# Output projection as three products of halves instead of one float32 product, in a transformer block on one core

## The chip, the cores and the metric

The kernel runs on one core of a Trainium2 chip. The metric is the device time of one execution in microseconds (us), lower is better. A core has five engines with a queue each: TensorE (PE; its weight loads are listed as PEld), VectorE (DVE), ScalarE (ACT), GpSimd (POOL) and SyncE (SP), which only starts DMAs here. Engines wait for each other by semaphores; every engine runs its own instructions in the order of the program.

## The reference, cut to what matters

Four sequences of 512 tokens with 128 channels pass an attention block and then a mixture of 160 experts. The change touches the last product of the attention, `a @ o_w.T`.

```python
h = _layernorm(x) * (1 + ca) + sa                       # x: 4 x 512 x 128
qkv = (h @ qkv_w.T).reshape(B, S, 3, 16, 64)            # 16 heads of 64
scores = einsum('bhqd,bhkd->bhqk', q, k) * scale + bias # relative-position bias
attn = softmax(scores, axis=-1)
a = einsum('bhqk,bhkd->bhqd', attn, v)
a = a.transpose(0, 2, 1, 3).reshape(B, S, 16 * 64)
x = x + ga * (a @ o_w.T)                                # the output projection
h = _layernorm(x) * (1 + cb) + sb
x = x + gb * experts(h)                                 # router, top 8 of 160, shared expert
```

## The kernel before, in words

The kernel has two stages. The attention takes the first half of the span, the experts the second; the change is in the attention.

The attention works on pairs of heads. For a sequence `b` there are eight pairs `n` (`HPAIRS`), and each pair has eight units `u` (`UNITS`): two heads by four tiles of 128 queries. One unit is a 128x512 tile of scores. Its way is: `scores` on TensorE (L409, L411) into one of two PSUM banks; `add_bias` on VectorE (L975), which takes the bias from `strips`, writes `prob` and the row minimum `nmax`; `exponential` on ScalarE (L706); `invert_sums` on VectorE (L992), for two units at a time; `normalise` on GpSimd (L858); `transpose_probs` on TensorE (L420); and a copy out of PSUM into `PT` (`copy_unit`, L204), by ScalarE for even units and by VectorE for odd ones. When the eight units of a pair are in `PT`, `attend` (L433) multiplies them by `v_sb`: a(n) in four steps `kb`, the result (128 rows of two heads, 512 tokens) standing in the one bank `BANK_O`. VectorE copies it to `oT` (`copy_o`, L998), and `project_out` (L446) adds its product with `woT[:, hp, :]` to `BANK_Y`. After the last pair of a sequence, `gate_y`, `transpose_y`, `update_x` and `new_statistics` bring the sum into `x_all`.

Nothing plans the order: it is written out by hand, one function `pair(b, n)` on each engine, and each engine's list is a program of its own. All lists overlap three pairs. In the list of `pair(b, n)`, by engine (S = scores, A = attend, T = transpose_probs, V = project_v, QK = project_qk, O = project_out; the numbers are units or steps `kb`):

- TensorE: S0 S1 of n | A2 A3 of n-2 | T4 T5 of n-1 | S2 S3 | V | O of n-2 | T6 T7 of n-1 | S4 S5 | A0 A1 of n-1 | T0 T1 of n | S6 S7 | QK of n+2 | T2 T3 of n.
- VectorE: bias 0, 1 | copy_o of n-2 | copy 5 of n-1 | sums 0 | bias 2, 3 | copy 7 of n-1 | sums 2 | bias 4, 5 | copy 1 | sums 4 | bias 6, 7 | copy 3 | sums 6 | qk_low (L958).
- ScalarE: exp 0, 1 | copy 4 of n-1 | exp 2, 3 | copy_v (L719) | copy 6 of n-1 | exp 4, 5 | copy 0 | exp 6, 7 | qk_high (L702) | copy 2.

Waits that touch the change: A0 of a pair waits until its units 6 (ScalarE) and 7 (VectorE) are copied and until `BANK_O` has been read (`s_o`). O waits for `s_o`. In `pair(b, 2)` of the second to fourth sequence, VectorE's `update_x` (L1018) and `new_statistics` (L1010) of the sequence before stand in the list ahead of `copy_o`.

The kernel has a number format that TensorE takes in one instruction per product, `float32r` (in the profile `fp32r`), beside plain float32, for which one product is two instructions in the profile. Where it is used, each operand is split into a rounded half and a rest, HIGH and LOW, and three products of halves are added (`PASSES`); the projections of q, k, v and the experts are done so already, with ScalarE writing HIGH and VectorE writing LOW as source minus HIGH. The output projection and `attend` are in plain float32.

In the notation of the profile, L446 is the output projection's matmul, L383 QK, L394 V, L998 `copy_o`.

Of the kernel before, what the change touches and what calls it, by code (L numbers as in the profile page):

```python
# [19 lines left out]
F32 = mybir.dt.float32  # L20
F32R = mybir.dt.float32r
# [3 lines left out]
P = 128  # L25
B, S, D = 4, 512, 128
# [8 lines left out]
HPAIRS = H // 2  # L35
# [4 lines left out]
HIGH, LOW = 0, 1  # L40
PASSES = ((HIGH, HIGH), (HIGH, LOW), (LOW, HIGH))


BANK_PROJ, BANK_S, BANK_T, BANK_O, BANK_Y = 0, 2, 4, 6, 7
# [11 lines left out]
def adaln_block(nc, x, emb, qkv_t, o_t, router_t, expert_bias, gate_t_in, down_t, gate_shared_t,  # L56
# [12 lines left out]
    with ctx:  # L69
        def sb(name, shape, dt=F32):  # L70
            return ctx.enter_context(nc.sbuf_tensor(name, shape, dt))

        def sem(name):
            return ctx.enter_context(nc.semaphore(name))

        ps = ctx.enter_context(nc.psum_tensor("ps", [P, 8, 512], F32))
# [1 line left out]
        ident = sb("ident", [P, P])  # L78
        x_all = sb("x_all", [P, B, QT * D])
        wT = sb("wT", [P, 2, QKV], F32R)  # L80
        woT = sb("woT", [P, HPAIRS, D])
        hT = sb("hT", [P, B, 2, S], F32R)
        hcur = sb("hcur", [P, 2, S], F32R)
        strips = sb("strips", [P, H * STRIP])
# [10 lines left out]
        v_sb = sb("v_sb", [P, 2, QT, 4 * HD])  # L95

        prob = sb("prob", [P, UNITS, S])
        oT = sb("oT", [P, 2, S])
        yT = sb("yT", [P, S])
        nmax = sb("nmax", [P, UNITS])  # L100
        rsum = sb("rsum", [P, UNITS])
# [50 lines left out]
        ld = {n: sem("ld_" + n) for n in ("ident", "c", "wmod", "emb", "onehot", "x0", "x", "qkv0", "qkv1", "ow",  # L152
                                          "small", "row", "strips0", "strips1", "strips2", "strips3", "strips4", "hcur")}
# [11 lines left out]
        s_s, s_ttr, s_exp, s_t = sem("scores"), sem("biased"), sem("exped"), sem("transposed")  # L165
        s_ca, s_cd = sem("copied_by_act"), sem("copied_by_dve")
        s_v, s_vc, s_pv = sem("v_projected"), sem("v_copied"), sem("pv_done")
        s_rinv, s_prob, s_o = sem("sums_inverted"), sem("normalised"), sem("o_copied")
        s_ymm, s_yg, s_ytr, s_x2 = sem("y_added"), sem("y_gated"), sem("y_transposed"), sem("x_updated")


# [50 lines left out]
        def _(sp):  # L222
# [54 lines left out]

            stack_pair(0, 0)
            load_strips(1)
            sp.dma_start(woT[:, :, :], o_t.rearrange("(n p) d -> p n d", p=P)).then_inc(ld["ow"], 16)  # L280
            stack_pair(0, 1)
            load_strips(2)
            load_strips(3)
# [64 lines left out]
        def _(pe):  # L348
# [3 lines left out]
            for half in range(2):  # L352
                nc.tensor.matmul(ps[0:H, BANK_PROJ + half, :], emb_sb, onehot[:, half * 512:(half + 1) * 512],
                                 start=True, stop=True).then_inc(row_mm, 1)
# [3 lines left out]
            for j in range(6):  # L358
                last = nc.tensor.matmul(ps[:, BANK_O, j * B:(j + 1) * B], wmod_sb[:, j * D:(j + 1) * D], cS[:, :],
                                        start=True, stop=True)  # L360
# [80 lines left out]
            def project_out(b, n):  # L441
                hp = n % HPAIRS
                pe.wait_ge(s_o, b * HPAIRS + (n + 1))
                if hp == 0:
                    pe.wait_ge(s_x2, b + (n // HPAIRS + X2_AHEAD))
                nc.tensor.matmul(ps[:, BANK_Y, :], woT[:, hp, :], oT[:, n % 2, :], start=hp == 0,  # L446
                                 stop=hp == HPAIRS - 1, skip_group_check=True).then_inc(s_ymm, 1)

            def transpose_y(b):

# [54 lines left out]
            pair(0, 0)  # L505
            pair(0, 1)
            pe.wait_ge(w_split, 6)
            pe.wait_ge(ld["ow"], 16)
            for b in range(B - 1):
                for n in range(2, HPAIRS + 2):  # L510
                    pair(b, n)
# [147 lines left out]
            for b in range(B):  # L659
# [3 lines left out]
                for t in range(QT):  # L663
                    last = nc.tensor.transpose(ps[:, BANK_G + b % 2, t * P:(t + 1) * P], hw[:, b, t * P:(t + 1) * P],
                                               ident[:, :])
# [4 lines left out]
        def _(act):  # L670
# [14 lines left out]
            def first_high(n):  # L685

                b = FIRST_ORDER[n]
                act.wait_ge(full_done, n + 1)
                nc.scalar.copy(hcur[:, HIGH, :] if b == 0 else hT[:, b, HIGH, :], h_full[b]).then_inc(grp_high, 1)
# [8 lines left out]
            def qk_high(b, n):  # L698
                act.wait_ge(s_qk, b * HPAIRS + (n + 1))
                if n >= 1:  # L700
                    act.wait_ge(s_stack[(n - 1) % 2], b * STACKED + PAIR_STACKED * ((n - 1) // 2 + 1))
                nc.scalar.copy(qkH[:, :, :], ps[:, BANK_PROJ:BANK_PROJ + 2, :]).then_inc(s_qkh, 1)  # L702
# [6 lines left out]
            def copy_probs(b, n, u):  # L709
                act.wait_ge(s_t, b * G + (UNITS * n + u + 1))  # L710
                if u == 0 and n >= 2:
                    act.wait_ge(s_pv, b * HPAIRS + (n - 1))
                copy_unit(nc.scalar.copy, n, u).then_inc(s_ca, 1)

            def copy_v(b, i):

                act.wait_ge(s_v, b * HPAIRS + (i + 1))
                half = i % 2
                nc.scalar.copy(v_sb[:, (i // 2) % 2, 2 * half:2 * half + 2, :].rearrange("p t n -> p (t n)"),  # L719
                               ps[:, BANK_PROJ + half, :]).then_inc(s_vc, 1)  # L720

            def pair(b, n, final=False):

                exponential(b, n, 0)
                exponential(b, n, 1)
                if n == 0:
                    qk_high(b, 1)
                if n >= 1:
                    copy_probs(b, n - 1, 4)

                exponential(b, n, 2)
                exponential(b, n, 3)
                if n == 0:
                    copy_v(b, 0)
                if not (final and n >= HPAIRS - 1):
                    copy_v(b, n + 1)
                if n >= 1:
                    copy_probs(b, n - 1, 6)

                exponential(b, n, 4)  # L740
                exponential(b, n, 5)
                if n == 0:
                    first_high(2)
                    first_high(3)
                copy_probs(b, n, 0)

                exponential(b, n, 6)
                exponential(b, n, 7)
                if not (final and n >= HPAIRS - 2):
                    qk_high(b, n + 2)  # L750
                copy_probs(b, n, 2)
# [11 lines left out]
                    pair(b, n)  # L763
            for n in range(2, HPAIRS):
                pair(B - 1, n, True)
            copy_probs(B - 1, HPAIRS - 1, 4)
            copy_probs(B - 1, HPAIRS - 1, 6)


            deviation(slice(0, NT), 3)  # L770
# [97 lines left out]
        def _(dve):  # L868
# [51 lines left out]
            def first_low(n):  # L920
                b = FIRST_ORDER[n]
                modulated_low(n, hcur if b == 0 else hT[:, b, :, :], h_full[b])
# [57 lines left out]
            def copy_probs(b, n, u):  # L980
                dve.wait_ge(s_t, b * G + (UNITS * n + u + 1))
                if u == 1 and n >= 2:
                    dve.wait_ge(s_pv, b * HPAIRS + (n - 1))
                copy_unit(nc.vector.tensor_copy, n, u).then_inc(s_cd, 1)
# [6 lines left out]
                    dve.wait_ge(s_prob, b * G + (g - UNITS + 2))  # L991
                nc.vector.reciprocal(rinv[:, u:u + 2], rsum[:, u:u + 2]).then_inc(s_rinv, 1)  # L992

            def copy_o(b, n):
                dve.wait_ge(s_pv, b * HPAIRS + (n + 1))
                if n >= 2:
                    dve.wait_ge(s_ymm, b * HPAIRS + (n - 1))
                nc.vector.tensor_copy(oT[:, n % 2, :], ps[:, BANK_O, :]).then_inc(s_o, 1)  # L998

            def gate_y(b):  # L1000

# [18 lines left out]
            def pair(b, n, final=False):  # L1020

                add_bias(b, n, 0)
                add_bias(b, n, 1)
                if n == 0:
                    first_low(1)
                    qk_low(b, 1)
                if n == 2 and b >= 1:
                    update_x(b - 1)
                    new_statistics(b - 1)
                if n >= 2:  # L1030
                    copy_o(b, n - 2)
                if n >= 1:
                    copy_probs(b, n - 1, 5)
                invert_sums(b, n, 0)

                add_bias(b, n, 2)
                add_bias(b, n, 3)
                if n == 0:
                    modulate(2)
                    modulate(3)  # L1040
                if n >= 1:
                    copy_probs(b, n - 1, 7)
                invert_sums(b, n, 2)

                add_bias(b, n, 4)
                add_bias(b, n, 5)
                if n == HPAIRS + 1:
                    gate_y(b)
                if n == 0:
                    qkv_low(3)  # L1050
                    qkv_low(4)
                    qkv_low(5)
                copy_probs(b, n, 1)
                invert_sums(b, n, 4)

                add_bias(b, n, 6)
                add_bias(b, n, 7)
                if n == 0:
                    first_low(2)
                    first_low(3)  # L1060
                copy_probs(b, n, 3)
                invert_sums(b, n, 6)
                if not (final and n >= HPAIRS - 2):
                    qk_low(b, n + 2)
# [13 lines left out]
                    pair(b, n)  # L1078
            for n in range(2, HPAIRS):
                pair(B - 1, n, True)  # L1080
            copy_o(B - 1, HPAIRS - 2)
            copy_probs(B - 1, HPAIRS - 1, 5)
            copy_probs(B - 1, HPAIRS - 1, 7)
            copy_o(B - 1, HPAIRS - 1)
            gate_y(B - 1)
            update_x(B - 1)
            new_statistics(B - 1)
# [3 lines left out]
            for n in range(NT):  # L1091
                last = nc.vector.bn_aggr(mv[:, n, :], stats[:, n, :])
# [144 lines left out]
```

## Time and profile before

| | us |
|---|---|
| median of 3 runs | 1002.72 (1000.67 to 1008.64) |
| profiled execution, its own time | 999.45 |
| profiled execution, span | 997.2 |
| PE busy in the span | 946.7 (95%) |
| DVE busy | 767.4 (77%) |
| ACT busy | 678.3 (68%) |
| POOL busy | 398.2 (40%) |

The span is the time between the first and the last instruction that the profiler saw, and 2.25 us of the execution lie around it. Busy times are unions of instructions, and matmuls overlap each other, so that a busy PE is not necessarily at its peak. The attention ends at about 505 us, the experts run from about 550 us to the end.

### The profile page before, as it was taken

The numbers are of one execution on the slowest core, as the hardware profiler recorded it, in microseconds if no ns is written. First come the engines' busy times: TensorE is split into PE (matmuls) and PEld (weight loads), VectorE is DVE, ScalarE is ACT, GpSimd is POOL, SyncE is SP. The second block draws the span as 40 slices with busy tenths as digits, with TensorE's granted clock in tenths as the row PEclk, the third lists the DMA queues.
The fourth block names the chain that finished last, engine by engine and source line by source line (L and its number), as shares of the span: only waits on it lengthen the run. The fifth ranks groups of instructions, "written<-read, shape, count | busy, mean of one in ns | idle before, by whom it ended". The sixth has DMA issues, their size and how long they took to land.

```text
span 997.2 us, 15699 instructions
## 1 busy us (share of the span) xinstructions
PE 946.7 (95%) x4592; PEld 685.8 (69%) x4592; DVE 767.4 (77%) x1452; ACT 678.3 (68%) x1168; POOL 398.2 (40%) x260
## 2 busy tenths in 40 slices
PE   4889999999999999999979699999999999999997
PEld 2546666666666666666524578888888888888886
DVE  5757667766676666767546689999999999999997
ACT  4656666666666666666536577777777777777775
POOL 0668888888888888888800000000000000000000
PEclk9999999999999999999979899999999999999999
DMA  7985445445553564355002999999999999999991
GB/s 210 274 224 125 97 118 127 117 95 128 128 120 81 117 149 110 82 128 127 22 0 75 213 218 221 220 220 223 222 221 225 221 222 223 222 222 222 222 208 43
DMA packets 71105, 160.57 MB, mean 161 GB/s; under 512 B 10272, under 2 KB 36192, under 8 KB 60944
## 3 DMA queue, kind: packets, MB, share of 16 engines
q1 hardware_dynamic: 71056, 159.97, 71.2%
q8 instruction: 24, 0.39, 0.2%
q14 instruction: 25, 0.20, 0.1%
HBM read 105.60 MB, written 2.42 MB: 108 GB/s over the span
## 4 chain that ended last, share of the span: by engine, by line
PE 84%; DMA 5%; DVE 4%; ACT 2%; POOL 2%; SPq 1%; issue 1%; POOLq 0%; ACTq 0%; DVEq 0%
PE ps L620 40%; PE ps L433 11%; PE ps L420 10%; PE ps L409 5%; PE ps L411 5%; PE ps L383 4%; PE ps L446 2%; PE ps L394 2%; POOL prob L858 2%; DMA strips<-in_L_ffn_w_down 2%; DMA k_low<-qk 2%; DVE prob L975 1%; DMA strips<-comb_rows 1%; DMA comb_rows<-strips 1%; PE ps L538 1%
## 5 line engine op out<-in xcount | busy, mean ns | idle before, releaser
L858 POOL TENSOR_SCALAR prob<-prob,rinv 128x512 f32<-128x512 f32 x256 | 398.1, 1568 | 96.4 <-DVE rinv L992 94.3
L706 ACT ACTIVATE prob<-prob,nmax 128x512 f32<-128x512 f32 x256 | 182.9, 715 | 139.5 <-DVE nmax L975 139.5
L620 PE MATMUL ps<-hT,wT 128*128 128x512 f32 x960 | 243.9, 390 | 0.3 <-DVE wT L1144 0.3
L1163 DVE TENSOR_TENSOR PT<-v_sb,strips 128x1024 f32<-128x1024 f32 x160 | 195.9, 1224 | 43.1 <-ACT v_sb L830 29.3
L830 ACT ACTIVATE v_sb<-ps 128x1024 f32<-128x1024 f32 x160 | 164.4, 1028 | 65.2 <-PE ps L620 65.1
L620 PE MATMUL ps<-stack,wT 128*128 128x512 f32 x640 | 198.4, 392 | 9.5 <-DVE wT L1150 9.5
L620 PEld LDWEIGHTS ps<-hT,wT 128*128 128x128 f32 x960 | 180.5, 188 | 38.9 <-ACT strips L805 1.1
L1150 DVE TENSOR_TENSOR wT<-PT,stack 128x1024 fp32r<-128x1024 f32 x160 | 195.0, 1219 | 0.0
L204 DVE COPY PT<-ps 128x512 f32<-128x512 f32 x128 | 88.5, 691 | 137.9 <-PE ps L420 135.2
L822 ACT CAST stack<-PT 128x1024 fp32r<-128x1024 f32 x160 | 166.6, 1041 | 9.5 <-DVE PT L1163 9.5
L420 PEld LDWEIGHTS ps<-ident,prob 128*128 128x128 f32 x1024 | 114.4, 140 | 75.9 <-POOL prob L858 50.9
L975 DVE CUSTOM_DVE_ANT_0 prob<-ps,strips 128x512 f32<-128x512 f32 x256 | 164.5, 680 | 2.7 <-PE ps L411 2.1
L620 PEld LDWEIGHTS ps<-stack,wT 128*128 128x128 f32 x640 | 120.1, 189 | 36.7 <-DVE wT L1150 12.1
L420 PE MATMUL ps<-ident,prob 128*128 128x128 f32 x1024 | 137.2, 276 | 2.8 <-ACT PT L204 1.6
L433 PE MATMUL ps<-PT,v_sb 128*64 128x512 f32 x512 | 124.4, 607 | 4.3 <-ACT PT L204 3.4
L409 PE MATMUL ps<-stack 128*128 128x512 f32 x256 | 112.7, 440 | 6.0 <-DMA k_low<-qk 5.8
L620 PE MATMUL ps<-wT 128*128 128x512 f32 x320 | 98.9, 391 | 0.0
L204 ACT COPY PT<-ps 128x512 f32<-128x512 f32 x128 | 74.0, 578 | 19.1 <-PE ps L420 19.0
L433 PEld LDWEIGHTS ps<-PT,v_sb 128*64 128x64 f32 x512 | 31.5, 137 | 64.7 <-issue 49.7
L620 PEld LDWEIGHTS ps<-wT 128*128 128x128 f32 x320 | 60.3, 189 | 12.6
L409 PEld LDWEIGHTS ps<-stack 128*128 128x128 f32 x256 | 48.8, 191 | 13.0 <-issue 4.0
L817 ACT CAST wT<-strips 128x256 fp32r<-128x256 f32 x80 | 32.3, 405 | 34.1 <-DMA strips<-in_L_ffn_w_down 33.9
(105 smaller groups left out, 742.8 us busy)
## 6 DMA issues: line engine op xcount, KB each, us to landing
strips<-comb_rows SPq DMA_DIRECT2D x158, 512.0 KB, 12.3
stack<-qk SPq DMA_DIRECT2D x128, 256.0 KB, 3.9
k_low<-qk SPq DMA_DIRECT2D x64, 128.0 KB, 3.9
hT<-qk SPq DMA_DIRECT2D x64, 128.0 KB, 3.8
strips<-bias_rows SPq DMA_DIRECT2D x3, 1792.0 KB, 14.7
strips<-in_L_ffn_w_gate SPq DMA_DIRECT2D x80, 64.0 KB, 10.4
strips<-in_L_ffn_w_down SPq DMA_DIRECT2D x80, 64.0 KB, 12.3
strips<-bias_rows SPq DMA_DIRECT2D x2, 896.0 KB, 5.3
```

The source lines that it names most:

```text
L204: return copy(dst[:, :, qt * P:(qt + 1) * P], ps[:, BANK_T + u % 2, :].rearrange("p (k s) -> p k s", s=P))
L409: nc.tensor.matmul(ps[:, BANK_S + g % 2, :], stack[:, par, head, 0, qt * P:(qt + 1) * P], stack[:, par, head, 1, :], start=True, stop=False)
L420: last = nc.tensor.transpose(ps[:, BANK_T + u % 2, kb * P:(kb + 1) * P], prob[:, u, kb * P:(kb + 1) * P], ident[:, :])
L433: last = nc.tensor.matmul(ps[head * HD:(head + 1) * HD, BANK_O, :], v_sb[:, (n // 2) % 2, kb, (n % 2) * P + head * HD:(n % 2) * P + (head ...
L620: last = nc.tensor.matmul(ps[:, bank + c, :], weights(a), rows(m, c), start=start and k == 0, stop=stop and k == 2, skip_group_check=True)
L706: nc.scalar.activation(prob[:, u, :], prob[:, u, :], ACT.Exp, bias=nmax[:, u:u + 1], scale=-1.0, accum_out=rsum[:, u:u + 1]).then_inc(s_ex ...
L822: nc.scalar.copy(h_high[:, k % 4, :], weighted[:, k % 4, :]).then_inc(s_hh, 1)
L830: nc.scalar.activation(silu[:, k % 2, :], ps[:, BANK_G + 2 * half:BANK_G + 2 * half + 2, :].rearrange("p c s -> p (c s)"), ACT.Silu).then_ ...
L858: nc.gpsimd.tensor_scalar(prob[:, u, :], prob[:, u, :], rinv[:, u:u + 1], None, ALU.mult).then_inc(s_prob, 1)
L975: nc.vector.tensor_tensor_reduce(out=prob[:, u, :], in0=ps[:, BANK_S + u % 2, :], in1=backwards, scale=-1.0, scalar=3.0e38, op0=ALU.add, o ...
L1150: nc.vector.tensor_tensor(h_low[:, k % 4, :], weighted[:, k % 4, :], h_high[:, k % 4, :].bitcast(F32), ALU.subtract).then_inc(s_hl, 1)
L1163: nc.vector.tensor_tensor(weighted[:, k % 4, :], silu[:, k % 2, :], cb[:, r, half * HALF:(half + 1) * HALF], ALU.mult).then_inc(s_mul, 1)
```

## The change

The attention's output is no longer copied out of `BANK_O` by VectorE alone. ScalarE writes the rounded half, `oT[.., HIGH, ..]` (`o_high`), and VectorE, when that is there, writes `BANK_O` minus that half (`o_low`). The weights of the projection are split in the same way, once, in `pair(0, 1)`, from the staging tile `o_in`. `project_out` becomes three matmuls in the rounded format. `o_high` stands in ScalarE's list of a pair after exp 1 and ahead of copy 4; `o_low` takes the place of `copy_o`. TensorE no longer waits for the load of the weights but, once, for their split. The size given for the DMAs' scratch memory in the constructor is 4096.

```diff
-        woT = sb("woT", [P, HPAIRS, D])
+        o_in = sb("o_in", [P, HPAIRS * D])
+        wo_parts = sb("wo_parts", [P, 2, HPAIRS * D], F32R)
-        oT = sb("oT", [P, 2, S])
+        oT = sb("oT", [P, 2, 2, S], F32R)
...
 def project_out(b, n):
                 pe.wait_ge(s_o, b * HPAIRS + (n + 1))
                 if hp == 0:
                     pe.wait_ge(s_x2, b + (n // HPAIRS + X2_AHEAD))
-                nc.tensor.matmul(ps[:, BANK_Y, :], woT[:, hp, :], oT[:, n % 2, :], start=hp == 0,
-                                 stop=hp == HPAIRS - 1, skip_group_check=True).then_inc(s_ymm, 1)
+                if b == 0 and n == 0:
+                    pe.wait_ge(s_wo, 1)
+                for k, (a, m) in enumerate(PASSES):
+                    last = nc.tensor.matmul(ps[:, BANK_Y, :], wo_parts[:, a, hp * D:(hp + 1) * D], oT[:, n % 2, m, :],
+                                            start=hp == 0 and k == 0, stop=hp == HPAIRS - 1 and k == 2,
+                                            skip_group_check=True)
+                last.then_inc(s_ymm, 1)
...
-            pe.wait_ge(ld["ow"], 16)
...
+            def o_high(b, n):
+                act.wait_ge(s_pv, b * HPAIRS + (n + 1))
+                if n >= 2:
+                    act.wait_ge(s_ymm, b * HPAIRS + (n - 1))
+                nc.scalar.copy(oT[:, n % 2, HIGH, :], ps[:, BANK_O, :]).then_inc(s_oh, 1)
...
                 exponential(b, n, 1)
                 if n == 0:
                     qk_high(b, 1)
+                if n >= 2:
+                    o_high(b, n - 2)
                 if n >= 1:
                     copy_probs(b, n - 1, 4)
...
+                if b == 0 and n == 1:
+                    act.wait_ge(ld["ow"], 16)
+                    nc.scalar.copy(wo_parts[:, HIGH, :], o_in[:, :]).then_inc(s_wo_high, 1)
                 copy_probs(b, n, 0)
...
+            o_high(B - 1, HPAIRS - 2)
             copy_probs(B - 1, HPAIRS - 1, 4)
             copy_probs(B - 1, HPAIRS - 1, 6)
+            o_high(B - 1, HPAIRS - 1)
...
-            def copy_o(b, n):
-                dve.wait_ge(s_pv, b * HPAIRS + (n + 1))
-                if n >= 2:
-                    dve.wait_ge(s_ymm, b * HPAIRS + (n - 1))
-                nc.vector.tensor_copy(oT[:, n % 2, :], ps[:, BANK_O, :]).then_inc(s_o, 1)
+            def o_low(b, n):
+                dve.wait_ge(s_oh, b * HPAIRS + (n + 1))
+                nc.vector.tensor_tensor(oT[:, n % 2, LOW, :], ps[:, BANK_O, :], oT[:, n % 2, HIGH, :].bitcast(F32),
+                                        ALU.subtract).then_inc(s_o, 1)
...
-                    copy_o(b, n - 2)
+                    o_low(b, n - 2)
...
+                if b == 0 and n == 1:
+                    dve.wait_ge(s_wo_high, 1)
+                    nc.vector.tensor_tensor(wo_parts[:, LOW, :], o_in[:, :], wo_parts[:, HIGH, :].bitcast(F32),
+                                            ALU.subtract).then_inc(s_wo, 1)
                 copy_probs(b, n, 3)
...
-    nc = bacc.Bacc("TRN2", target_bir_lowering=False, num_devices=1)
+    nc = bacc.Bacc("TRN2", target_bir_lowering=False, num_devices=1, dynamic_dma_scratch_size=4096)
```

## Rows read from the trace of the kernel before

**Rows 1.** The page: the span, the engines' busy times, TensorE's granted clock in 40 slices.

```profile
span 997.2 us, 15699 instructions
PE 946.7 (95%) x4592; PEld 685.8 (69%) x4592; DVE 767.4 (77%) x1452; ACT 678.3 (68%) x1168; POOL 398.2 (40%) x260
...
PEclk9999999999999999999979899999999999999999
```

**Rows 2.** Groups by line and shape: shapes xcount | busy us, mean ns | idle before.

```profile
L446 PE MATMUL ps<-oT,woT 128*128 128x512 f32 x64 | 33.1, 598 | 0.8 <-DVE oT L998 0.8
...
L719 ACT COPY v_sb<-ps 128x512 f32<-128x512 f32 x32 | 17.9, 563 | 0.0
...
L1018 DVE TENSOR_TENSOR x_all<-x_all,ps 128x512 f32<-128x512 f32 x4 | 2.7, 683 | 0.7 <-PE ps L453 0.7
```

**Rows 3.** Timeline of one regular pair: start us, duration us, engine, line [idle before].

```profile
256.74 1.94 PE L433 MATMUL ps<-PT,v_sb 128*64 128x512 f32 x8
...
259.74 0.69 DVE L204 COPY PT<-ps 128x512 f32<-128x512 f32 x1 [1.84 <-PE ps L420]
...
260.47 1.54 PE L383 MATMUL ps<-hcur,wT 128*128 128x512 f32 x6
...
261.85 1.04 PE L420 MATMUL ps<-ident,prob 128*128 128x128 f32 x8
...
262.56 0.99 ACT L702 CAST qk<-ps 128x1024 fp32r<-128x1024 f32 x1
...
263.61 1.21 DVE L958 TENSOR_TENSOR qk<-ps,qk 128x1024 fp32r<-128x1024 f32 x1
...
264.73 0.68 DVE L975 CUSTOM_DVE_ANT_0 prob<-ps,strips 128x512 f32<-128x512 f32 x1
...
265.94 0.69 DVE L998 COPY oT<-ps 128x512 f32<-128x512 f32 x1
...
266.88 0.56 ACT L204 COPY PT<-ps 128x512 f32<-128x512 f32 x1
...
267.42 0.67 DVE L975 CUSTOM_DVE_ANT_0 prob<-ps,strips 128x512 f32<-128x512 f32 x1
...
268.13 0.72 ACT L706 ACTIVATE prob<-prob,nmax 128x512 f32<-128x512 f32 x1 [0.69 <-DVE nmax L975]
268.16 1.02 PE L446 MATMUL ps<-oT,woT 128*128 128x512 f32 x2
...
269.02 1.04 PE L420 MATMUL ps<-ident,prob 128*128 128x128 f32 x8
...
270.91 1.94 PE L433 MATMUL ps<-PT,v_sb 128*64 128x512 f32 x8
```

**Rows 4.** Timeline of pair 2 of the second sequence.

```profile
180.83 0.56 ACT L204 COPY PT<-ps 128x512 f32<-128x512 f32 x1
...
181.40 0.68 DVE L998 COPY oT<-ps 128x512 f32<-128x512 f32 x1
...
182.66 0.68 DVE L975 CUSTOM_DVE_ANT_0 prob<-ps,strips 128x512 f32<-128x512 f32 x1
...
185.91 1.94 PE L433 MATMUL ps<-PT,v_sb 128*64 128x512 f32 x8 [0.85 <-ACT PT L204]
```

**Rows 5.** Timeline of pair 1 of the first sequence.

```profile
53.68 0.59 ACT L204 COPY PT<-ps 128x512 f32<-128x512 f32 x1 [1.09 <-PE ps L420]
...
57.30 0.69 DVE L204 COPY PT<-ps 128x512 f32<-128x512 f32 x1 [1.22 <-PE ps L420]
```

**Rows 6.** Timeline of the attention's end.

```profile
476.39 18.51 POOL L858 TENSOR_SCALAR prob<-prob,rinv 128x512 f32<-128x512 f32 x12 [0.71 <-DVE rinv L992]
...
500.14 0.69 DVE L998 COPY oT<-ps 128x512 f32<-128x512 f32 x1 [3.79 <-PE ps L433]
500.88 1.12 PE L446 MATMUL ps<-oT,woT 128*128 128x512 f32 x2 [0.79 <-DVE oT L998]
```

**Rows 7.** The DMA queues: packets, MB, share of 16 engines.

```profile
q1 hardware_dynamic: 71056, 159.97, 71.2%
```

More of the change, by code:

```diff
@@ L167, in adaln_block @@
         s_v, s_vc, s_pv = sem("v_projected"), sem("v_copied"), sem("pv_done")
-        s_rinv, s_prob, s_o = sem("sums_inverted"), sem("normalised"), sem("o_copied")
+        s_rinv, s_prob, s_o = sem("sums_inverted"), sem("normalised"), sem("o_split")
+        s_oh, s_wo_high, s_wo = sem("o_high"), sem("wo_high"), sem("wo_split")
         s_ymm, s_yg, s_ytr, s_x2 = sem("y_added"), sem("y_gated"), sem("y_transposed"), sem("x_updated")
@@ L279, in _ @@
             load_strips(1)
-            sp.dma_start(woT[:, :, :], o_t.rearrange("(n p) d -> p n d", p=P)).then_inc(ld["ow"], 16)
+            sp.dma_start(o_in[:, :].rearrange("p (n d) -> p n d", d=D), o_t.rearrange("(n p) d -> p n d", p=P)).then_inc(ld["ow"], 16)
             stack_pair(0, 1)
@@ L1080, in _ @@
                 pair(B - 1, n, True)
-            copy_o(B - 1, HPAIRS - 2)
+            o_low(B - 1, HPAIRS - 2)
             copy_probs(B - 1, HPAIRS - 1, 5)
             copy_probs(B - 1, HPAIRS - 1, 7)
-            copy_o(B - 1, HPAIRS - 1)
+            o_low(B - 1, HPAIRS - 1)
             gate_y(B - 1)
```

## The prediction

> **What bounds the kernel now.** I read the page first: TensorE is busy 95% of the span, VectorE 77%, ScalarE 68%, and the granted clock is at its upper level, 2.4 GHz, in nearly every slice [rows 1]. The edit is in the attention, so I then read one regular pair of the timeline [rows 3]. From A0 of one pair (256.74) to A0 of the next (270.91) it takes 14.17 us, and none of TensorE's rows there has an idle time before it: TensorE sets the pace, and what its own list loses is time won, as long as nobody else becomes later than it. How late the others may become is the question, so the last view is the pair in which VectorE is late already, pair 2 of the second sequence [rows 4], where TensorE stands for 0.85 us ahead of A0 until ScalarE's copy into `PT` (unit 6) is done.
>
> **Part 1, the three products.** The old product, two instructions, takes from 268.16 to the start of T6 at 269.02: 0.86 us [rows 3]. Six products in the rounded format, QK, take from 260.47 to 261.85: 1.38 us, 0.23 each [rows 3]. Three take 0.69, a saving of 0.17 us on TensorE. There are 32 products (64 instructions [rows 2]): 5.4 us, if all of it shows.
>
> **Part 2, the split of the output.** VectorE's own work doesn't change: the copy took 0.69 us [rows 3], and a VectorE operation on PSUM and a second tensor of this size took 0.683 [rows 2]. ScalarE gets one more operation. No row shows just this one, a 128x512 cast out of PSUM; a copy of that size out of PSUM took 0.563 [rows 2], a cast of twice the size 0.99 [rows 3]. I take 0.56, the nearest in size, and keep 0.99 as the far end; nothing speaks for less than 0.56.
>
> What matters is where it stands. `copy_o` ran at 265.94, right after bias 1 [rows 3]. `o_low` has to wait for `o_high`, and `o_high` stands behind exp 0 and exp 1, which can't be before bias 0 and 1. ScalarE ended exp 1 at 266.88, where copy 4 starts [rows 3]. So `o_high` runs 266.88 to 267.44, and with 0.06 us from ScalarE's end to VectorE's start (262.56 + 0.99 to 263.61 [rows 3]) `o_low` starts at 267.50, 1.56 us later than `copy_o`. VectorE stands in that time, and behind the waiting instruction are copy 5, sums 0, bias 2, bias 3, copy 7.
>
> From the start of `copy_o` to bias 2 it takes 1.26 us when nothing else is waited for (181.40 to 182.66 [rows 4]); in the regular pair it took 1.48 (265.94 to 267.42 [rows 3]), since copy 5 had to wait for T5. Bias 2 therefore starts at 267.50 + 1.26 = 268.76 and is 1.34 us late. ScalarE had 0.69 us idle ahead of exp 2, which ends in waiting for bias 2 [rows 3]; `o_high` itself fits in that, the lateness of bias 2 does not. Behind bias 2 stand exp 2, exp 3, `copy_v` and copy 6 on ScalarE, and A0 waits for copy 6. Rows 4 price that chain as a whole: bias 2 at 182.66, A0 at 185.91 and released by ScalarE's copy, 3.25 us. In the regular pair there are 3.49 us between them (267.42 to 270.91 [rows 3]). So 0.24 us of lateness are free, and the rest moves A0: 1.34 - 0.24 = 1.10 us.
>
> Does the next pair give it back? No: the chain is a closed loop. A0 A1 and T0 T1 of a pair release copy 1 (VectorE idle 1.84 us ahead of 259.74, for TensorE [rows 3]); then bias 6, exp 6, exp 7, `qk_high` (262.56), `qk_low` (263.61), bias 0 (264.73), exp 0, exp 1 (to 266.88), and now `o_high`, `o_low`, copy 5, bias 2, exp 2, exp 3, `copy_v`, copy 6, A0. Every link starts right behind the one before, so the loop takes 14.17 + 1.10 = 15.27 us, and the 0.17 us of part 1 lie in the shadow of it: TensorE comes early to a wait that ends when ScalarE is done. The product itself isn't late by much: `o_low` ends at 268.19, and TensorE would come at 268.16.
>
> **How often.** Pairs 2 to 9 of three sequences and 2 to 7 of the last have an `o` in their list, 30. In three of them (pair 2 of sequences two to four) VectorE does `update_x` and the statistics first; exp 1 ends at 180.83, `o_low` could start at 180.83 + 0.62 = 181.45, and `copy_o` started at 181.40 [rows 4]: 0.05 us each, taken as 0.2 in all. The last pair comes apart too: GpSimd works without a break from 476.39 on for twelve units, 18.51 us, to 494.90 [rows 6], and what VectorE is late behind that costs little; between 0 and 1.1, I take 0.3. That leaves 26 regular pairs: 26 x 1.10 = 28.6 us. At the end of the attention the chain stands free: `copy_o` at 500.14, the product at 500.88 [rows 6]; `o_high` and the hand-over put 0.62 ahead, the shorter product takes 0.17 away: +0.45.
>
> **Part 3, the weights.** ScalarE splits 128x1024 once, ahead of copy 0 of pair 1, where it was idle 1.09 us; the cast of that size took 0.99 [rows 3, 5]. VectorE's part stands ahead of copy 3, with 1.22 us idle, for an operation like the one of 1.21 [rows 3, 5]. Taken as nothing; without the cover it is 2.2 us, once. `o_in` is filled by the same transfer as `woT` was, at the same place in SP's list, which is not moved past anything.
>
> **Part 4, the scratch size.** All but a hundredth of the data goes over one queue of the kind hardware_dynamic [rows 7], issued by SP; I see no user of the scratch and take 0. No row prices it otherwise. The Trainium skill (SBUF — State Buffer, section on SBUF size) says that the scratch holds the descriptors of the software path, which would make it 0 as well; no run here shows that yet.
>
> **The sum.** 28.6 + 0.2 + 0.3 + 0.45 = 29.6 us on the profiled execution: 999.45 + 29.6 = 1029. That execution lies 3.3 us below the median of the runs, 1002.72, so the forecast for the median is 1032. The ends: with a cast of 0.99 us in place of 0.56 each regular pair costs 1.53, which gives 1044; with a hand-over or a slack that is 0.3 us kinder, 0.8 a pair, 1024.
>
> **The rivals.**
> A. TensorE keeps the pace. Mechanism: bias 2 is late by 0.24 us or less, or ScalarE makes the lateness good before copy 6, so that A0 stays bound by TensorE's list; then the 5.4 us of part 1 show: 1002.7 - 5.4 + 0.5 = 998. For it speaks that TensorE has no idle time in the regular pair and that ScalarE has 0.69 us idle at this place. Against it: 1.34 is far over 0.24, and rows 4 show this very chain holding TensorE. It would need `o_high` to start some 1.1 us earlier than the end of exp 1, which the list forbids. The Trainium skill (Perfetto Trace Analysis, Identifying the Most-Contended Engine) has the rule to find the engine with the highest occupancy and to optimise it first. By that rule the result is A. For the pace before the change the trace agrees, with TensorE at 95%; for what one more link in the loop does the rule has no term.
> B. The stops let the clock fall. TensorE now stands over 1 us in each pair. If that brought the lower level, 1.2 GHz, the part of the loop on TensorE, from A0 at 256.74 to copy 1 at 259.74, 3.0 us [rows 3], would up to double. In a third of 30 pairs that is another 30 us: 1062. Against it: TensorE stood 0.85 us at 185.91 [rows 4], and the slices about there (184 us is the eighth of forty) were granted 9 tenths or more [rows 1].
>
> **Chances.** Forecast 0.83, A 0.10, B 0.05, something else 0.02. About 1% (10 us) is what a measurement of this kernel can tell from no change. Slower by over 1%: forecast and B, 0.87, as the forecast's own ends are both past 1013. Within 1%: A and half of what is left, 0.11. Faster by over 1% would need twice the saving of part 1: 0.02. The range is the forecast with its two ends, opened by 4 us below and 2 above for the spread of the runs before, 1000.67 to 1008.64: 1020 to 1046.
>
> **What would show each step.** In the profile of the changed kernel: (1) L446 with 96 instructions and 0.69 to 0.75 us from the first to T6. (2) `o_low` 0.06 us behind the end of `o_high`, VectorE idle about 1.5 us ahead of it, with ScalarE as releaser. (3) A0 with some 1.1 us idle on TensorE, released by ScalarE's copy, in 26 pairs, and 15.3 us from A0 to A0. (4) ScalarE idle about 1.5 us ahead of exp 2 (copy 4 ends at 268.00, exp 2 starts 0.71 us behind bias 2, at 269.47), released by bias 2. (5) The experts' stage as long as before. Wrong would be the prediction if A0's idle time is missing (A), if L433 and L420 last twice as long in some pairs (B), or if the cast is much longer than 0.56.

## The result and the profile after

The changed kernel takes 1036.89 us, median of 6 runs (1030.17 to 1042.52); the kernel before 1003.29 (1000.67 to 1008.64). The ratio is 1.0341, 95% interval 1.031 to 1.0373. The profiled execution took 1030.17 us, 30.7 more than the 999.45 of before. Forecast were 1032 (1029 against the profiled execution) and 1020 to 1046.

The page of the changed kernel, the lines that answer to [rows 1]:

```profile
span 1028.4 us, 15796 instructions
PE 949.6 (92%) x4624; PEld 695.2 (68%) x4624; DVE 775.2 (75%) x1453; ACT 696.3 (68%) x1201; POOL 398.2 (39%) x260
...
PEclk9999999999999999999988899999999999999999
```

No engine is busier by more than 18 us, and that one is ScalarE, which has 33 casts more (32 `o_high` and the split of the weights). TensorE's busy time grew by 2.9 us, the span by 31.2, and its share fell from 95% to 92%. So it is not mainly work that was added, it is time in which TensorE stands. The clock is granted as before.

The groups by line and shape that answer to [rows 2]. In the changed kernel L451 is the projection's matmul (L446 before), L725 `o_high`, L1015 `o_low`, L435 `attend`, L422 the transposes, L994 `add_bias`, L712 the exponential, L206 the copies into `PT`, L731 `copy_v`:

```profile
L451 PE MATMUL ps<-oT,wo_parts 128*128 128x512 f32 x96 | 30.8, 429 | 2.3 <-DVE oT L1015 2.2
...
L725 ACT CAST oT<-ps 128x512 fp32r<-128x512 f32 x32 | 18.1, 566 | 5.5 <-PE ps L435 5.5
...
L1015 DVE TENSOR_TENSOR oT<-ps,oT 128x512 fp32r<-128x512 f32 x32 | 22.1, 692 | 44.7 <-ACT oT L725 44.7
```

VectorE stood 44.7 us ahead of `o_low`, in 29 of its 32 times, for ScalarE's `o_high`; `copy_o` stood 4.6 us in all, three times, and each time for TensorE. The regular pair that answers to [rows 3]:

```profile
272.13 1.94 PE L435 MATMUL ps<-PT,v_sb 128*64 128x512 f32 x8 [1.01 <-ACT PT L206]
...
280.12 0.68 DVE L994 CUSTOM_DVE_ANT_0 prob<-ps,strips 128x512 f32<-128x512 f32 x1
...
282.28 0.56 ACT L725 CAST oT<-ps 128x512 fp32r<-128x512 f32 x1
...
282.88 0.69 DVE L1015 TENSOR_TENSOR oT<-ps,oT 128x512 fp32r<-128x512 f32 x1 [1.45 <-ACT oT L725]
...
283.62 0.96 PE L451 MATMUL ps<-oT,wo_parts 128*128 128x512 f32 x3
...
284.15 0.67 DVE L994 CUSTOM_DVE_ANT_0 prob<-ps,strips 128x512 f32<-128x512 f32 x1
...
284.42 1.03 PE L422 MATMUL ps<-ident,prob 128*128 128x128 f32 x8
...
284.87 0.72 ACT L712 ACTIVATE prob<-prob,nmax 128x512 f32<-128x512 f32 x1 [1.54 <-DVE nmax L994]
...
286.30 0.56 ACT L731 COPY v_sb<-ps 128x512 f32<-128x512 f32 x1
...
286.76 0.58 ACT L206 COPY PT<-ps 128x512 f32<-128x512 f32 x1
...
287.39 1.94 PE L435 MATMUL ps<-PT,v_sb 128*64 128x512 f32 x8 [1.01 <-ACT PT L206]
```

Two numbers of such a pair carry all that follows. From bias 0 (280.12) to bias 2 (284.15) there are 4.03 us, where before there were 2.69 (264.73 to 267.42 [rows 3]): bias 2 is 1.34 us late. From A0 to A0 (272.13 to 287.39) there are 15.26 us instead of 14.17. In between one sees the path: VectorE idle 1.45 ahead of `o_low`, ScalarE idle 1.54 ahead of exp 2 for bias 2, TensorE idle 1.01 ahead of A0 for ScalarE's copy 6. The later product is not a second path to A0: T6 and T7, which stand behind it, are done at 285.45 (284.42 + 1.03), and copy 6 starts only at 286.76, right behind `copy_v`. The list of the changed kernel's waits between 100 and 480 us has the first and the last of these as (who waited, for whom: us in total, times, longest):

```profile
DVE oT L1015 <- ACT oT L725: 31.9, 22, 1.5
...
PE ps L435 <- ACT PT L206: 25.3, 25, 1.0
```

Over the whole attention TensorE has 29 such stops of 1.00 to 1.02 us ahead of A0: 26 in regular pairs, and three in pair 2 of the later sequences, where it stood 0.85 before.

### The profile page after: what moved, and what is told of

Same layout as the page of the kernel before. It is cut to its first block, busy times and chain, and to the rows that moved or that the text cites. A ratio compares the mean times of both kernels' runs of the same rounds, so it can differ in the third digit from the quotient of the medians.

```text
span 1028.4 us, 15796 instructions
## 1 busy us (share of the span) xinstructions
PE 949.6 (92%) x4624; PEld 695.2 (68%) x4624; DVE 775.2 (75%) x1453; ACT 696.3 (68%) x1201; POOL 398.2 (39%) x260
## 4 chain that ended last, share of the span: by engine, by line
PE 74%; ACT 9%; DVE 7%; DMA 4%; issue 3%; SPq 2%; POOL 1%; DVEq 0%; POOLq 0%; ACTq 0%
PE ps L626 40%; PE ps L435 11%; PE ps L422 8%; ACT prob L712 5%; PE ps L385 4%; PE ps L411 4%; PE ps L413 4%; DVE prob L994 2%; DVE PT L206 2%; DMA k_low<-qk 2%; DMA strips<-in_L_ffn_w_down 1%; ACT PT L206 1%; ACT v_sb L731 1%; POOL prob L877 1%; DMA comb_rows<-strips 1%
## 5 line engine op out<-in xcount | busy, mean ns | idle before, releaser
L712 ACT ACTIVATE prob<-prob,nmax 128x512 f32<-128x512 f32 x256 | 182.9, 716 | 137.4 <-DVE nmax L994 137.2
L849 ACT ACTIVATE v_sb<-ps 128x1024 f32<-128x1024 f32 x160 | 164.6, 1029 | 81.1 <-PE ps L626 80.8
L206 DVE COPY PT<-ps 128x512 f32<-128x512 f32 x128 | 88.2, 689 | 113.0 <-PE ps L422 111.4
L994 DVE CUSTOM_DVE_ANT_0 prob<-ps,strips 128x512 f32<-128x512 f32 x256 | 165.2, 683 | 3.5 <-PE ps L413 2.2
L422 PEld LDWEIGHTS ps<-ident,prob 128*128 128x128 f32 x1024 | 114.4, 140 | 63.1 <-POOL prob L877 49.6
L435 PE MATMUL ps<-PT,v_sb 128*64 128x512 f32 x512 | 124.4, 607 | 31.5 <-ACT PT L206 30.7
L422 PE MATMUL ps<-ident,prob 128*128 128x128 f32 x1024 | 136.9, 276 | 2.5 <-ACT PT L206 1.6
L206 ACT COPY PT<-ps 128x512 f32<-128x512 f32 x128 | 74.4, 581 | 34.0 <-PE ps L422 34.0
L435 PEld LDWEIGHTS ps<-PT,v_sb 128*64 128x64 f32 x512 | 31.5, 137 | 93.9 <-issue 49.8
L1015 DVE TENSOR_TENSOR oT<-ps,oT 128x512 fp32r<-128x512 f32 x32 | 22.1, 692 | 44.7 <-ACT oT L725 44.7
```

Of the source, the lines that this page charges most:

```text
L206: return copy(dst[:, :, qt * P:(qt + 1) * P], ps[:, BANK_T + u % 2, :].rearrange("p (k s) -> p k s", s=P))
L422: last = nc.tensor.transpose(ps[:, BANK_T + u % 2, kb * P:(kb + 1) * P], prob[:, u, kb * P:(kb + 1) * P], ident[:, :])
L435: last = nc.tensor.matmul(ps[head * HD:(head + 1) * HD, BANK_O, :], v_sb[:, (n // 2) % 2, kb, (n % 2) * P + head * HD:(n % 2) * P + (head ...
L712: nc.scalar.activation(prob[:, u, :], prob[:, u, :], ACT.Exp, bias=nmax[:, u:u + 1], scale=-1.0, accum_out=rsum[:, u:u + 1]).then_inc(s_ex ...
L849: nc.scalar.activation(silu[:, k % 2, :], ps[:, BANK_G + 2 * half:BANK_G + 2 * half + 2, :].rearrange("p c s -> p (c s)"), ACT.Silu).then_ ...
L994: nc.vector.tensor_tensor_reduce(out=prob[:, u, :], in0=ps[:, BANK_S + u % 2, :], in1=backwards, scale=-1.0, scalar=3.0e38, op0=ALU.add, o ...
```

## The experiments

Theory L is that of the prediction: the pairs form a closed loop, VectorE's wait for ScalarE makes bias 2 late, and what exceeds 0.24 us is added to every regular pair. Rival P blames what is new on TensorE, rival S the amount of ScalarE's new work wherever it stands. Lateness of bias 2 is measured in each trace from bias 0 to bias 2, less 2.69. The edits are shown shortened: declarations and the calls behind the last pair are left out. "Ratio" is always against the kernel before, measured in the same series.

**E1, the wait alone**, put into the kernel before.

```diff
+ def o_high(b, n):                       # ScalarE, behind exp 1
+     act.wait_ge(s_pv, b * HPAIRS + (n + 1))
+     nc.scalar.copy(o_spare[:, :], ps[:, BANK_O, :]).then_inc(s_oh, 1)
  def copy_o(b, n):
-     dve.wait_ge(s_pv, b * HPAIRS + (n + 1))
+     dve.wait_ge(s_oh, b * HPAIRS + (n + 1))
```

> Edit of the kernel before: ScalarE copies BANK_O into a spare tile after exp 1, and VectorE's copy_o waits for that; the single float32 product stays. Theory L (the loop: bias 2 is late because VectorE waits for ScalarE): 15.26 us from A0 to A0 as in the changed kernel, 0.8 to 1.1 us idle on TensorE ahead of A0, about 30 us over before, 1033. Rival P (what is new on TensorE, three products with three weight loads, costs the time): no change, 1003, 14.17 us from A0 to A0.

Measured: 1029.12 us against 1003.28 (ratio 1.0248, 1.0188 to 1.0309). The timeline of a regular pair (L435 is `attend`, L985 bias, L1008 `copy_o`):

```profile
271.86 1.94 PE L435 MATMUL ps<-PT,v_sb 128*64 128x512 f32 x8 [0.85 <-ACT PT L206]
...
279.85 0.68 DVE L985 CUSTOM_DVE_ANT_0 prob<-ps,strips 128x512 f32<-128x512 f32 x1
...
282.59 0.69 DVE L1008 COPY oT<-ps 128x512 f32<-128x512 f32 x1 [1.44 <-ACT o_spare L719]
...
283.87 0.67 DVE L985 CUSTOM_DVE_ANT_0 prob<-ps,strips 128x512 f32<-128x512 f32 x1
...
287.11 1.94 PE L435 MATMUL ps<-PT,v_sb 128*64 128x512 f32 x8 [0.84 <-ACT PT L206]
```

Without any of the three products the loop is that of the changed kernel: bias 2 late by 1.33, 15.25 us from A0 to A0. TensorE stands 0.84 here and 1.01 there since its old product is longer; the spacing is the same, so the shorter product only lengthens the stop. P is out. The median lies 4 us under the 1033 that was expected, 25.8 over before instead of 30; the profiled executions are 30.1 apart (1029.51 and 999.45).

**E2, the three products alone**, in the changed kernel.

```diff
- o_high on ScalarE; o_low waits for it and writes the rest
+ def o_low(b, n):                        # VectorE, at copy_o's place
+     nc.vector.tensor_copy(oT[:, n % 2, HIGH, :], ps[:, BANK_O, :]).then_inc(s_o, 1)
- ... oT[:, n % 2, m, :]
+ ... oT[:, n % 2, HIGH, :]
```

> Edit of the changed kernel: VectorE writes the rounded half at copy_o's old place and nobody writes the rest; both halves are read from it, so the three products are there and the result leaves the rest out. ScalarE does nothing for it. Theory L: TensorE sets the pace, 0.06 to 0.17 us less than 14.17 from A0 to A0, 2 to 5 us under before, 998 to 1001. Rival P: slower than before by 10 us or more.

Measured: 998.2 us, ratio 0.9949 (0.9915 to 0.9984). TensorE's timeline:

```profile
269.69 1.94 PE L435 MATMUL ps<-PT,v_sb 128*64 128x512 f32 x8
...
281.10 0.85 PE L451 MATMUL ps<-oT,wo_parts 128*128 128x512 f32 x3
281.80 1.03 PE L422 MATMUL ps<-ident,prob 128*128 128x128 f32 x8
...
283.69 1.94 PE L435 MATMUL ps<-PT,v_sb 128*64 128x512 f32 x8
```

The three products take 0.70 us up to T6 (forecast 0.69, before 0.86), there is no stop ahead of A0, and the pair takes 14.00, 0.17 less. The gain of part 1 exists, about 5 us in all by the medians (1003.28 and 998.2), when nobody else is late.

**E3, both halves by VectorE**, in the changed kernel.

```diff
  def o_low(b, n):
-     dve.wait_ge(s_oh, b * HPAIRS + (n + 1))
+     dve.wait_ge(s_pv, b * HPAIRS + (n + 1))
+     nc.vector.tensor_copy(oT[:, n % 2, HIGH, :], ps[:, BANK_O, :]).then_inc(s_oh, 1)
+     dve.wait_ge(s_oh, b * HPAIRS + (n + 1))
```

> Edit of the changed kernel: VectorE writes both halves, one after the other, at copy_o's old place; ScalarE has nothing to do with it. VectorE has 0.6 us more work than in the changed kernel, ScalarE 0.57 less. Theory L: bias 2 is late by one operation and a hand-over, 0.68 us, less 0.24 free: 0.44 a pair, 14.6 us from A0 to A0, +11 us, 1014. Rival S (the added ScalarE operation costs, wherever it stands): no ScalarE operation, so 1003 or a little less.

Measured: 1011.34 us, ratio 1.0061 (1.0027 to 1.0095); by the medians 8 us over before, between the 11 of theory L and the 0 of rival S. The trace decides: bias 0 at 284.34, bias 2 at 287.56, late by 0.53, and A0 at 276.36 and 290.80, 14.44 apart, with TensorE waiting 0.35 for copy 6 though ScalarE has no new operation at all. S, which wanted 14.17 or less, is out. I had said 0.68 late: the second operation starts 0.72 behind the first, but I forgot to take off the 0.19 us that copy 5 waits for T5 anyway; 0.72 - 0.19 = 0.53.

**E4, the same work, moved**, in the changed kernel.

```diff
  ScalarE:  exp 0, exp 1, - o_high - copy 4, + o_high + exp 2, ...
  VectorE:  bias 0, 1, - o_low - copy 5, sums 0, bias 2, 3, + o_low + copy 7, ...
  TensorE:  S2 S3, V, - O - T6 T7, S4 S5, + O + A0 A1, ...
```

> Edit of the changed kernel, with all its work: o_high behind copy 4 (where ScalarE waits for bias 2), o_low behind bias 3 (where VectorE waits for T7), the product behind S5, just ahead of A0. Nobody in the loop waits for them. Theory L: TensorE sets the pace again, 14.0 to 14.1 us from A0 to A0, 998 to 1001, a little under before. Rival S: 18 us of ScalarE's work show, 1020.

Measured: 995.71 us, ratio 0.9946 (0.9912 to 0.998). Timeline:

```profile
270.50 1.94 PE L435 MATMUL ps<-PT,v_sb 128*64 128x512 f32 x8
...
281.10 0.58 ACT L725 CAST oT<-ps 128x512 fp32r<-128x512 f32 x1
...
281.88 0.72 ACT L712 ACTIVATE prob<-prob,nmax 128x512 f32<-128x512 f32 x1 [0.20 <-DVE nmax L994]
...
282.38 0.69 DVE L1015 TENSOR_TENSOR oT<-ps,oT 128x512 fp32r<-128x512 f32 x1
...
283.72 0.85 PE L451 MATMUL ps<-oT,wo_parts 128*128 128x512 f32 x3
...
284.50 1.94 PE L435 MATMUL ps<-PT,v_sb 128*64 128x512 f32 x8
```

`o_high` now lies in ScalarE's wait for bias 2, of which 0.20 us are left, `o_low` starts without a wait, and TensorE sets the pace: 14.00 from A0 to A0. By their medians the same instructions take 41 us less than in the order of the change (1036.89), and the version is faster than both kernels. It is 2 us under the range that was expected. What I had left out is pair 2 of the later sequences: `o_low` no longer stands ahead of bias 2 there, where VectorE is late already, and that pair takes 15.06 us from A0 to A0 (171.40 to 186.46) instead of 15.66; there are three of them.

**E5, E6, E7, `o_high` at three other places** of ScalarE's list, in the changed kernel: behind copy 4, between exp 0 and exp 1, ahead of exp 0. They were measured against 1001.2 us of the kernel before.

```diff
  E5:  exp 0, exp 1, - o_high - copy 4 + o_high +, exp 2, ...
  E6:  exp 0, + o_high + exp 1, - o_high - copy 4, ...
  E7:  + o_high + exp 0, exp 1, - o_high - copy 4, ...
```

> Edit of the changed kernel: o_high one place later on ScalarE, behind copy 4. Theory L: o_low and bias 2 are 0.46 us later than in the changed kernel, and each regular pair with them: 15.7 us from A0 to A0, 12 us over the changed kernel, 1049. Rival S (it is the amount of ScalarE's work): no change, 1037.

> Edit of the changed kernel: o_high one place earlier, between exp 0 and exp 1. Theory L: o_low 0.72 us earlier, so bias 2 too: 14.5 to 14.6 us from A0 to A0, 18 us under the changed kernel, 1015. Rival S: no change, 1037.

> Edit of the changed kernel: o_high ahead of exp 0. It starts when A3 is done, exp 0 and 1 are 0.7 us later than now and with them sums 0, which comes ahead of bias 2: bias 2 late by 0.3 to 0.45 against before, 14.25 to 14.4 us from A0 to A0, 1005 to 1009. Rival S: no change against the changed kernel, 1037.

Measured: E5 1046.66 us (ratio 1.0463, 1.0383 to 1.0544), E6 1012.88 (1.011, 1.0073 to 1.0147), E7 1011.84 (1.0113, 1.0076 to 1.015). E5's timeline:

```profile
278.15 1.94 PE L435 MATMUL ps<-PT,v_sb 128*64 128x512 f32 x8 [1.01 <-ACT PT L206]
...
286.14 0.68 DVE L994 CUSTOM_DVE_ANT_0 prob<-ps,strips 128x512 f32<-128x512 f32 x1
...
290.12 0.96 PE L451 MATMUL ps<-oT,wo_parts 128*128 128x512 f32 x3 [0.39 <-DVE oT L1015]
...
290.64 0.67 DVE L994 CUSTOM_DVE_ANT_0 prob<-ps,strips 128x512 f32<-128x512 f32 x1
...
293.89 1.94 PE L435 MATMUL ps<-PT,v_sb 128*64 128x512 f32 x8 [1.01 <-ACT PT L206]
```

Here `o_low` is so late that TensorE stands for it too, 0.39 us ahead of the product; ahead of A0 it still waits for ScalarE's copy 6.

E7's timeline, where my forecast of 14.25 to 14.4 was 0.08 short:

```profile
270.46 0.59 ACT L725 CAST oT<-ps 128x512 fp32r<-128x512 f32 x1 [1.70 <-PE ps L435]
...
271.08 0.69 DVE L1015 TENSOR_TENSOR oT<-ps,oT 128x512 fp32r<-128x512 f32 x1 [0.32 <-ACT oT L725]
...
272.49 0.17 DVE L1011 RECIPROCAL rinv<-rsum 128x2 f32<-128x2 f32 x1
...
272.69 0.69 DVE L994 CUSTOM_DVE_ANT_0 prob<-ps,strips 128x512 f32<-128x512 f32 x1
```

There `o_high` waits for A3 and holds up exp 0 and 1, so that sums 0 (272.49), which needs exp 1, comes late and bias 2 with it. S wanted no change in all three. With the same instructions the time moved by -25 to +10 us against the changed kernel by the medians, which come from different series, and by -22 to +14 us by the profiled executions (1007.72, 1012.46 and 1044.21 against 1030.17). Put in a row, with 14.17 + (late - 0.24) beside what was measured from A0 to A0:

| kernel | bias 2 late, measured | 14.17 + (late - 0.24) | A0 to A0, measured |
|---|---|---|---|
| E3 | 0.53 | 14.46 | 14.44 |
| E7 | 0.55 | 14.48 | 14.48 |
| E6 | 0.63 | 14.56 | 14.55 |
| E1 | 1.33 | 15.26 | 15.25 |
| changed kernel | 1.34 | 15.27 | 15.26 |
| E5 | 1.81 | 15.74 | 15.74 |

The slack of 0.24, read from one disturbed pair of the trace of before, holds over the whole row to 0.02 us. What the row tests is that the two other pieces of the loop do not change: from A0 to bias 0 it takes 7.98 to 7.99 us in all of these kernels, and from bias 2 to the next A0 3.24 to 3.26. The lateness itself is measured here, and forecast only ahead of each run.

**E8, ScalarE's operation alone**, in the kernel before, from SBUF, with nobody waiting.

```diff
+ nc.scalar.copy(o_spare[:, :], wT[:, HIGH, 0:512].bitcast(F32))     # ScalarE, behind exp 1
```

> Edit of the kernel before: ScalarE gets one more 128x512 cast at the place of o_high, behind exp 1, from a constant SBUF tile into a spare one; nobody waits for it, and copy_o and the product are as before. Theory L: it fits in the 0.69 us in which ScalarE waits for bias 2, 14.17 us from A0 to A0, no change, 1003. Rival S (ScalarE's added work costs): 32 times 0.57 us, 18 us over before, 1021.

Measured: 1001.05 us against 1001.63, ratio 1.0002 (0.9966 to 1.0037). Timeline:

```profile
266.79 0.60 ACT L719 CAST o_spare<-wT 128x512 fp32r<-128x512 f32 x1
...
267.34 0.67 DVE L985 CUSTOM_DVE_ANT_0 prob<-ps,strips 128x512 f32<-128x512 f32 x1
...
268.05 0.72 ACT L708 ACTIVATE prob<-prob,nmax 128x512 f32<-128x512 f32 x1 [0.17 <-DVE nmax L985]
```

ScalarE's idle time ahead of exp 2 shrinks from 0.69 to 0.17 and swallows the operation; from A0 to A0 there are 14.16 to 14.20 us, as in the kernel before. With E1 at the same place this separates the two: the operation costs nothing, VectorE's wait for it costs all. E8 reads from SBUF and not from PSUM as `o_high` does; that the read from PSUM costs nothing either is seen in E4, which has it.

## Why the prediction was right, step by step

**Part 1.** 0.69 for three products: 0.70 in E2. In the changed kernel it is 0.80 (283.62 to 284.42), over the 0.75 that the prediction's first sign allowed, and hidden. There the first of the three weight loads starts together with the product, at 283.62; in E2 it starts 0.12 us ahead of it, at 280.98. That the saving stays in the shadow of the wait is shown by E1 against the changed kernel: 15.25 and 15.26.

**Part 2.** `o_high` 0.56 forecast, 0.566 measured; the far end, 0.99, was not needed. Hand-over 0.06 forecast, 0.04 measured (282.28 + 0.56 to 282.88). Bias 2 late 1.34 and 1.34. From `o_low` to bias 2 1.26 and 1.27, from bias 2 to A0 3.25 and 3.24. The pair 15.27 and 15.26.

**How often.** The 26 regular pairs are there, as counted. The end of the attention: `o_high` starts at 530.35 where `copy_o` started at 500.14, and the product at 531.72 where it was 500.88 [rows 6], 30.8 later. The rows of the changed kernel:

```profile
530.35 0.59 ACT L725 CAST oT<-ps 128x512 fp32r<-128x512 f32 x1 [5.19 <-PE ps L435]
...
531.72 0.97 PE L451 MATMUL ps<-oT,wo_parts 128*128 128x512 f32 x3 [1.40 <-DVE oT L1015]
```

From the first of the two to the second it is 1.37 instead of 0.74, 0.63 more for 0.62 forecast. Of the 30.8 us, 1.2 arose before any `o`: S0 of pair 2 of the first sequence started at 62.21 instead of 61.01. Of these, 0.87 were there at the first A0 (51.99 instead of 51.12), before the first operation of the weights' split (53.37), and E1, which has no split, started the same S0 at 62.06; E2 to E7 started it between 61.30 and 62.60. In the traces of before and of E1 a wait for a transfer ends there; what moves it stays open. The other 29.6 stand against 28.6 + 0.2 + 0.3 + 0.62 = 29.7 of the forecast. The parts fit less closely than the sum: up to the last regular A0 (502.15 instead of 472.54) 28.4 came about, for 28.6 + 0.2, and from there to `o_high` 0.6, for 0.3, within the 0 to 1.1 that were given. Behind that the last product is 0.15 us shorter (0.97 for 1.12), for 0.17. The pair of [rows 4] came out as unchanged, 15.68 us from A0 to A0 for 15.66 before.

**Parts 3 and 4.** The split of the weights is hidden, as said: ScalarE's copy 0 behind it starts at 54.55 instead of 53.68, late by the 0.87 us that were there before it, and VectorE's copy 3 at 58.18 instead of 57.30, late by 0.88. Behind the start of the last product there are 496.7 us of span, 496.3 before: the experts' stage did not change, and the scratch size shows no cost or gain in it; no run changes it alone. The sentence of the Trainium skill (SBUF — State Buffer, section on SBUF size) on what the scratch is for agrees with this trace as far as times can tell, and these can't show more than that nothing was lost.

**What did not fit.** The medians differ by 33.6 us, the profiled executions by 30.7, and the profiled one was the fastest of the six. I have no trace of the slower ones. E1, with the same loop, had a median of 1029.12 and its four runs within 4 us. Whether the last 3 us are the kernel's or the chip's in those runs stays open. The median came out 5 us over its forecast, the profiled execution 1 us over its own. A slip in the chances: forecast and B make 0.88, not 0.87.

**The rivals.** A needed a lateness under 0.24; 1.34 was measured. The rule of the Trainium skill (Perfetto Trace Analysis, Identifying the Most-Contended Engine) did give the pace of before, and E2 and E4 paid as it says, with TensorE the busiest engine; in the changed kernel TensorE still is the busiest at 92%, and its work no longer sets the time. B, a falling clock, did not come about: the mean granted clock is 0.988 in the profiled executions of both kernels, in the changed one with 29 stops of about 1.01 us.

## What to carry to other kernels

Before handing one engine's operation over to two, ask where the first half can start at the earliest in its engine's list, and what stands behind the waiting half; here a free operation on ScalarE and one of unchanged length on VectorE cost 30 us, since VectorE stood 1.5 us with the next pair's bias behind it. Look for a pair or round of the trace in which something is late already: it gave both the slack (0.24 us) and the length of the chain (3.25 us), and with the lateness of bias 2 they give the loop of six kernels, six orders or splits of nearly the same work, to 0.02 us. When the halves have to exist, put each where its engine waits anyway and the consumer behind both: the same instructions then gained half a per cent.

## What the runs showed of the hardware that I had not expected

In E3 an operation of VectorE that reads what the one before it wrote, with a semaphore between them, started 0.72 us behind it (285.56 to 286.28 below). In E1, `copy_o` and copy 5, of which the second doesn't need the first, are 0.61 apart (282.59 to 283.20). The second operation starts 0.03 us behind the end of the first where it needs it (285.56 + 0.69 to 286.28), and 0.08 ahead of that end where it doesn't (282.59 + 0.69 to 283.20), about 0.1 us between the two. Measured in the same way, from end to start, the hand-over from ScalarE to VectorE takes 0.03 to 0.04. So a hand-over between two engines is no dearer here than one within VectorE; what it cost was the place of the first half in ScalarE's list. No run tells the semaphore from the read of the fresh data.

```profile
285.56 0.69 DVE L1007 CAST oT<-ps 128x512 fp32r<-128x512 f32 x1
286.28 0.69 DVE L1009 TENSOR_TENSOR oT<-ps,oT 128x512 fp32r<-128x512 f32 x1
```
